# Cross-attention with layer norms on one core: all 34 batch turns of all five engines written out instead of 30 of them in a loop

## The reference, cut to what matters

```python
qn  = layer_norm(q,  q_norm_g,  q_norm_b)
kvn = layer_norm(kv, kv_norm_g, kv_norm_b)
Q = (qn  @ Wq).reshape(B, N_q,  16, 32).transpose(0, 2, 1, 3)
K = (kvn @ Wk).reshape(B, N_kv, 16, 32).transpose(0, 2, 1, 3)
V = (kvn @ Wv).reshape(B, N_kv, 16, 32).transpose(0, 2, 1, 3)
attn = softmax(einsum('bhqd,bhkd->bhqk', Q, K) / sqrt(32))
ctx  = einsum('bhqk,bhkd->bhqd', attn, V)          # back to (B, N_q, 512)
out  = q + gelu(ctx @ Wo + bo)
```

## Time and profile before

| | before |
|---|---|
| median of three runs | 3278.94 us |
| span of the profiled execution | 3277.9 us |
| instructions in the span | 60424 |
| TensorE matmuls, busy | 3244.4 us (99%), x16611 |
| TensorE weight loads, busy | 2140.0 us (65%) |
| VectorE, ScalarE, GpSimd busy | 69%, 69%, 71% |
| share of the DMA engines' time | 60.2% (queue q1) |
| PEclk in the 40 slices | 9 in all of them (90% of full speed or more) |

### The profile page before, as it was taken

The page is one execution under the profiler, slowest core; times in us unless marked ns, Lnnn a source line. Parts: engine busy times, 40 slices in busy tenths (PEclk is TensorE's granted clock), DMA queues, the critical chain, the costliest instruction groups (busy, mean ns, idle before and its releaser), DMA issues.

```text
span 3277.9 us, 60424 instructions
## 1 busy us (share of the span) xinstructions
PE 3244.4 (99%) x16611; PEld 2140.0 (65%) x16611; DVE 2256.6 (69%) x4769; ACT 2276.0 (69%) x3985; POOL 2315.9 (71%) x1544
## 2 busy tenths in 40 slices
PE   8999999999999999999999999999999999999998
PEld 5566666666666666666666666666666666666664
DVE  6667667676676676666766766766667667667664
ACT  5677666777767777667767667776777676677765
POOL 3676776777677767777776677777767776777665
PEclk9999999999999999999999999999999999999999
DMA  6655656566556556565665566565656655666653
GB/s 142 89 106 106 107 103 113 90 108 106 105 102 103 108 106 105 103 116 87 110 107 103 105 100 109 107 102 103 119 83 111 106 106 106 98 109 106 103 78 76
DMA packets 186492, 340.15 MB, mean 104 GB/s; under 512 B 20561, under 2 KB 20577, under 8 KB 186466
## 3 DMA queue, kind: packets, MB, share of 16 engines
q1 hardware_dynamic: 186000, 339.03, 60.2%
q10 hardware_dynamic: 466, 0.80, 0.2%
HBM read 104.87 MB, written 33.55 MB: 42 GB/s over the span
## 4 chain that ended last, share of the span: by engine, by line
PE 97%; DVE 1%; ACT 1%; issue 1%; DMA 0%; POOL 0%; SPq 0%; ACTq 0%; POOLq 0%; DVEq 0%
PE gen L856 43%; PE score L883 15%; PE score L876 15%; PE ctx L903 14%; PE gen L847 4%; PE gen L943 4%; PE gen L965 1%; DVE maxes L706 0%; DMA k_stack<-k_nat 0%; ACT q_stack L617 0%; PE score L788 0%; DVE stats L725 0%; ACT probs L563 0%; PE gen L837 0%; POOL probs L475 0%
## 5 line engine op out<-in xcount | busy, mean ns | idle before, releaser
L475 POOL TENSOR_TENSOR probs<-probs 128x1024 f32<-128x1024 f32 x762 | 1802.0, 2396 | 291.9 <-PE ctx L903 285.7
L706 DVE TENSOR_REDUCE maxes<-score 128x1 f32<-128x512 f32 x2048 | 1295.8, 682 | 202.8 <-PE score L883 201.9
L563 ACT ACTIVATE probs<-score 128x512 f32<-128x512 f32 x2048 | 1086.3, 621 | 140.5 <-PE score L876 134.4
L883 PE MATMUL score<-k_stack,q_stack 96*128 96x512 f32 x2048 | 762.1, 413 | 3.4 <-DVE maxes L706 1.8
L876 PE MATMUL score<-q_stack,k_stack 128*128 128x512 f32 x2048 | 697.8, 407 | 6.3 <-ACT q_stack L617 6.3
L883 PEld LDWEIGHTS score<-k_stack,q_stack 96*128 96x128 f32 x2048 | 378.9, 189 | 217.6 <-ACT probs L563 83.9
L876 PEld LDWEIGHTS score<-q_stack,k_stack 128*128 128x128 f32 x2048 | 374.5, 189 | 200.8 <-DVE maxes L706 59.3
L903 PE MATMUL ctx<-probs,v_sb 128*32 128x512 f32 x4096 | 492.6, 599 | 0.0
L856 PE MATMUL gen<-w_v,cT 128*128 128x512 f32 x1536 | 462.2, 396 | 0.0
L856 PE MATMUL gen<-cT,w_k 128*128 128x512 f32 x1536 | 461.9, 400 | 0.2 <-DVE q_nat L688 0.2
L856 PE MATMUL gen<-xT,w_q 128*128 128x512 f32 x1536 | 448.6, 394 | 3.0 <-issue 0.4
(11 more groups left out here) (89 smaller groups left out, 2765.7 us busy)
## 6 DMA issues: line engine op xcount, KB each, us to landing
k_stack<-k_nat SPq DMA_DIRECT2D x384, 256.0 KB, 7.8
q_stack<-q_nat SPq DMA_DIRECT2D x381, 256.0 KB, 5.6
tok<-in_x SPq DMA_DIRECT2D x132, 256.0 KB, 10.4
tok<-in_ctx SPq DMA_DIRECT2D x128, 256.0 KB, 11.0
res<-in_x SPq DMA_DIRECT2D x124, 256.0 KB, 2.6
out<-res SPq DMA_DIRECT2D x124, 256.0 KB, 2.1
probs<-in_L_xattn_Wq SPq DMA_DIRECT2D x1, 1024.0 KB, 8.1
probs<-in_L_xattn_Wk SPq DMA_DIRECT2D x1, 1024.0 KB, 10.4
```

Of the source, the lines that this page charges most:

```text
L475: pool.tensor_tensor(probs[:, c + 1, heads], probs[:, c + 1, heads], probs[:, c, heads], ALU.add).then_inc(pool_added, 1)
L563: act.activation(probs[:, n, part, :], score_at(s, "st", i)[:], ACT.Exp, scale=SCALE).then_inc(exp_done, 1)
L706: dve.tensor_reduce(maxes[:, u1 % 2, SROW + i:SROW + i + 1], score_at(s, "s", i)[:], AX_X, ALU.max, negate=True).then_inc(max_done, 1)
L883: pe.matmul(score_bank(pe, b, s, "s", i)[:, :], q_stack[0:KROWS, u1 % 2, n, P * part:P * (part + 1)], k_stack[0:KROWS, u1 % 2, n, :], star ...
```

## The change

`all_batches` runs over the same 34 turns in the same order, as a Python loop, so that every turn is written into each engine's program with constants. The bodies of the turns, their items, and what is computed are the same. Each wait compares with a constant, each DMA has a fixed address, and no branch is left in the engines' own code. The program of each engine is as long as what it executes.

```diff
         def all_batches(eng, batch):
 
-            batch(-1)
-            batch(0)
-            with eng.Fori(1, B - 1) as b:
+            for b in range(-1, B + 1):
                 batch(b)
-            batch(B - 1)
-            batch(B)
```

## The result

The changed kernel took 3265.39 us (median of four runs, 3264.91 to 3266.09) beside 3280.01 us for the kernel before: the ratio is 0.9953, 95% interval 0.9939 to 0.9967. Measured again on another occasion it was 3264.12 us beside 3280.20, ratio 0.9951 (0.9937 to 0.9964). So 14.6 and 16.1 us are gained, where 18.0 were forecast. The time itself is 4.5 us above the forecast 3260.9 us, 1.1 us of which is the kernel before, which took 3280.01 us here and not 3278.94. The profiled span is 3263.3 us, 14.6 less than before.

What follows compares the result with a forecast made beforehand. TensorE's matmuls, covering 99% of the span, were taken to bound the kernel. Branch 10.8, chain after step 0 5.1 and chain after step 2 2.1 sum to 18.0 us, giving 3260.9 us from 3278.94; range 3253 to 3270 us.

Steps and rivals of the forecast that it cites:

- The branch: TensorE's gap at the end of each looped turn: shrinks from 0.42 to 0.06 us, 10.8 us in all.
- The form of turn 0: Gap of 0.06 us between turns -1 and 0, with no loop instruction; all 31 places were to take it.
- The chain after step 0: Chain of the maxima from `m` to first score: two handoffs with constant waits save 0.17 us a turn, 5.1 us.
- ScalarE's handoff: After step 0, from `m` to `max_cut`: 0.44 us in the loop, 0.36 with constants, so 0.08 us saved.
- The chain after step 2: Chain of the maxima after step 2: only `max_hl` has the late second value, 0.07 us a turn, 2.1 us.
- Fetching: Instruction fetches in every written-out turn: cost taken as 0, upper bound 1.5 us, with turn 1 as test.
- (a): Rival: only the turn's gap goes, other engines make up the handoffs; 3268.1 us, chance 0.14.
- (b): Rival: the stall after the row sums or other near misses dissolve too; 3254.3 us, chance 0.08.
- the stall after the row sums: Step 2: a score matmul takes 0.42 us to the next; taken as 0 gain, 6.6 us if wholly gone.
- (c): Rival: no change, TensorE enters step 0 earlier but waits for VectorE or ScalarE; 3276 us, chance 0.05.
- (d): Rival: slower through late instruction fetches, 112 blocks of 1.2 us exposed cost 134 us; 3395 us, chance 0.09.

Runs made afterwards that it cites:

- e6: Changed kernel plus unread extra matmuls in three idle places of turns -1 and 0, the bank's wait placed first in all turns; 3267.43 us beside 3280.20 for the kernel before.
- e9: Changed kernel plus unread extra matmuls in idle places of turns -1 and 0, old wait order in other turns; 3263.04 us beside 3281.70 for the kernel before.
- e1: Kernel before with only TensorE's turns written out, the other engines looped; 3267.82 us beside 3280.85, ratio 0.9962.
- e8: Kernel before with VectorE alone written out; 3276.69 us beside 3280.20, ratio 0.9990.
- e10: Kernel before with TensorE and VectorE written out, ScalarE, GpSimd and SP queue looped; 3261.86 us beside 3281.70, ratio 0.9941.
- e2: Kernel before with all engines but TensorE written out; 3276.37 us beside 3280.85, ratio 0.9987.
- e7: Changed kernel with 64 unused semaphore increments at the start of ScalarE's and VectorE's programs; 3263.76 us beside 3280.20 for the kernel before, ratio 0.9955.
- e3: Kernel before with only ScalarE and VectorE written out; 3276.29 us beside 3280.85, ratio 0.9986.

## Why the prediction came out as it did

The direction, the places and the median turn (99.72 us; 99.7 to 99.8 forecast) were right, and the time lies in the range. The gain was 14.6 to 16.1 us, not 18.0. That the median turn came out so exactly is in part luck: it lost 0.61 us for 0.60 forecast, but the term of one chain was too big by about as much as those of the other two places were too small. Step by step:

- **The branch.** Forecast 0.42 to 0.06 us a jump. It became 0.08 to 0.09 at all turns but turn 0. The form of turn 0 was the wrong pick of the three by 0.025 us, 0.8 us in sum; why it is shorter there is open, and the longer stall ahead of that `m` is not the reason, since in e6 and e9, where extra matmuls fill the stall, the gap is 0.03 us. The gaps gave 10.1 us for 10.8 forecast. That the gap is kept and not taken back later was right (e1): the first stretch shrank by 0.39 us, 0.04 more than the gap.
- **The chain after step 0.** Forecast 3.80 us from `m` to the first score for 3.93, measured 3.82. I gave 0.08 us to ScalarE's handoff and 0.09 to VectorE's, added them to 0.17, and held that ScalarE couldn't take the gain back. The second stretch shrank by 0.10 us only, 3.1 us for the 5.1 forecast. VectorE's 0.09 is all there (e8); of ScalarE's 0.08 some 0.02 count, since TensorE has other products until then. The pair of scores did fall to 0.67 us, but that was no gain beside the earlier start.
- **The chain after step 2.** Forecast 0.07 us, from `max_hl` alone, 2.1 us in sum. TensorE's own second value was late as well; e1 gets 0.08 us without VectorE. Where both are constant, 3.81 us remain of 3.92, and the fourth stretch shrank by 0.12 us, 3.7 us in sum. Without ScalarE's constants it shrinks by 0.17 (e10).
- **Fetching.** Costed at nothing, with a bound of 1.5 us. It costs 1.8 us in the changed kernel, in six turns. I read turn 1 as the test of fetching, and it was too small a sample: a crossing costs only when it meets an idle engine, and a late restack only where no slack is left. The rule of the Trainium skill that I had as a rival, in "Runtime: NRT & Kernel Launch", section "Instruction fetch mechanics" (crossing a block is mostly hidden), holds in these runs with a number for its exception: 0.14 to 0.37 us on ScalarE or VectorE. The price of a whole block, 1.2 us, is never paid.
- **The ends of the kernel.** Not in my sum at all. I held head, turn 0 and drain to be equal, as their programs are. Turn 0 varies by 2 to 3 us with TensorE's clock.
- **The rivals.** (a) fell with e2 and e8: the handoffs are worth 4.5 and 3.5 us by themselves, 0.17 to 0.19 us a turn. (b) fell: the stall after the row sums in the earlier trace rows is 0.43 us in the median of the turns after and 0.45 before. (c) fell with e1. (d) was right in kind and off in size by a factor of some 75 (134 us for 1.8).

## What to carry to other kernels

Where one engine is at 99%, look for the few places where its queue is empty or where it waits for a chain through other engines: only there a branch, a computed value or a semaphore instruction has a price. Here one branch and three or four waits of a turn made nearly all of the gain (0.57 of 0.61 us), and the other computed values of the turn, some ninety on TensorE alone, next to nothing: the third stretch of the turn, which has waits of the same kind, lasts the same in all forms. A kernel that already has turns in both forms gives these prices without a run, to within 0.07 us a turn each. Two delays on one chain don't add up where the engine at its end has other work until the later one is over. Write out the engines that lie on the path, here two of five. Writing out the others bought nothing here; it brings fetches, which now and then stop an idle engine, and for ScalarE a worse order of two waits. It is the blocks of TensorE, which has to be written out, that delay a DMA that someone needs.

## What the runs showed of the hardware that I had not expected

- A sequencer that reaches a certain place of its program with nothing queued stands 0.34 to 0.37 us (VectorE) or 0.14 to 0.28 us (ScalarE). The places are alike modulo 128 instructions, about what one fetched packet of these engines holds (8 KB: 0.99 MB / 121), and the pauses moved to other items when 64 instructions were put ahead (e7).
- A 16 KB instruction fetch delays restacks of 256 KB that run at the same time by 1 to 2 us (7.0 us to 9.0 for the last one of q in turn 11).
- A taken loop branch on TensorE's sequencer lasts 0.21 us, on the four other engines 0.04 to 0.07 by the same view of the kernel before.
- With two waits on an instruction, it matters which stands last: the late one should be the one that the instruction itself carries (about 0.06 us on TensorE in e6, 0.06 on ScalarE in e3).
- The same program ran its turn 0 at full clock from 60.3 us on in one execution and at half clock for 3.4 us in another.
